# A decoder layer's second cross-attention stream: the query tiles of a quad are taken in the order 0, 7, 1, 6, 2, 5, 3, 4

## What is computed

```python
x = _layernorm(x + _L0_attn_ref(x, wq, wk, wv, wo, rel_emb))     # 16 heads of 64, relative bias
x = _layernorm(x + _L0_xattn_ref(x, ctx, ctx, Wq, bq, Wk, bk, Wv, bv, Er))
x = _layernorm(x + _L0_ffn_ref(x, Wg, bg, w1, b1, w2, b2, w3, b3))  # 16 experts, 128 tokens each
```

```python
QEr = jnp.einsum('bhsd,ld->bhsl', q, Er_s)
Srel = _skew(QEr)
QK = jnp.einsum('bhsd,bhtd->bhst', q, k)
attn = (QK + Srel) / math.sqrt(dh)
attn = jnp.where(causal[None, None], attn, -jnp.inf)
attn = jax.nn.softmax(attn, axis=-1)
out = jnp.einsum('bhst,bhtd->bhsd', attn, v)
```

## Time and profile before

| | us |
|---|---|
| median of three runs | 4421.03 |
| the profiled execution | 4421.36 |
| its span | 4419.6 |
| second stream in the first batch, from its first scores | 704.9 to about 909.6 |
| its quads 1 to 4 by windows | 54.6, 48.0, 48.1, 48.0 |

### The profile page before, as it was taken

How to read it: one execution, slowest core, us unless ns; L and a number is a source line. 1 busy time by engine, 2 the same in 40 slices (tenths; PEclk the granted TensorE clock), 3 DMA queues, 4 the chain that set the end, 5 groups by cost and what they waited for, 6 DMA issues and landing times. The chain is left out here.

```text
span 4419.6 us, 90910 instructions
## 1 busy us (share of the span) xinstructions
PE 3878.7 (88%) x36922; PEld 2372.6 (54%) x36922; DVE 2499.9 (57%) x4789; ACT 1573.0 (36%) x3188; POOL 908.0 (21%) x1023
## 2 busy tenths in 40 slices
PE   6999987899999878999998789999988819999992
PEld 3667544556665346566653566766545504444441
DVE  3777435777773357777723677777246762222224
ACT  2444135744441357444413674444137600000000
POOL 2333101123330011233300112333001102222220
PEclk8999999999999989999999899999998959999996
DMA  8333258634332686333327853433278414454445
GB/s 252 109 90 90 87 222 308 201 104 113 90 85 86 261 293 196 94 109 96 98 76 285 283 168 112 119 95 106 77 281 278 152 60 121 109 132 116 130 114 171
DMA packets 286223, 659.45 MB, mean 149 GB/s; under 512 B 24336, under 2 KB 90816, under 8 KB 282576
## 3 DMA queue, kind: packets, MB, share of 16 engines
q1 hardware_dynamic: 270160, 616.08, 43.2%
q0 software_dynamic: 15344, 35.46, 4.2%
q10 hardware_dynamic: 320, 2.23, 0.1%
HBM read 384.84 MB, written 210.11 MB: 135 GB/s over the span
## 5 line engine op out<-in xcount | busy, mean ns | idle before, releaser
L504 ACT ACTIVATE sc<-sc,nmax 128x1024 f32<-128x1024 f32 x516 | 591.7, 1147 | 797.6 <-DVE nmax L730 797.2
L461 POOL TENSOR_SCALAR sc<-sc,pinv 128x1024 f32<-128x1024 f32 x516 | 577.4, 1120 | 1230.0 <-DVE pinv L738 1217.2
L860 DVE CUSTOM_DVE_ANT_0 sc<-psum,big 128x896 f32<-128x896 f32 (+7 forms) x512 | 362.1, 754 | 217.5 <-PE psum L1221 170.7
L1039 PE MATMUL psum<-pts,wct 32*64 32x256 f32 x8192 | 458.6, 376 | 3.9 <-issue 3.9
L1039 PE MATMUL psum<-xall,wct 32*64 32x256 f32 x8192 | 457.6, 376 | 0.0
L1024 PE MATMUL psum<-xt,w_all 128*128 128x256 f32 x1792 | 415.7, 385 | 23.4 <-PEq L1021 23.4
L504 ACT ACTIVATE sc<-sc,xmax 128x896 f32<-128x896 f32 (+7 forms) x512 | 394.1, 772 | 49.8 <-DVE xmax L860 45.4
L755 DVE STREAM_TRANSPOSE pts<-sc 128x1024 f32<-128x1024 f32 (+3 forms) x342 | 333.6, 975 | 131.4 <-PE psum L1039 87.6
L1024 PEld LDWEIGHTS psum<-xt,w_all 128*128 128x128 f32 x1792 | 332.5, 190 | 128.2 <-issue 66.8
L730 DVE CUSTOM_DVE_ANT_0 sc<-psum,table_a 128x1024 f32<-128x1024 f32 x258 | 312.5, 1211 | 130.1 <-PE psum L986 114.2
L1039 PEld LDWEIGHTS psum<-pts,wct 32*64 32x64 f32 x8192 | 309.5, 132 | 100.8 <-issue 49.9
(11 more groups left out here) (160 smaller groups left out, 5553.0 us busy)
## 6 DMA issues: line engine op xcount, KB each, us to landing
wct<-xall SPq DMA_DIRECT2D x576, 128.0 KB, 2.4
big<-skew_d SPq DMA_DIRECT2D x48, 1024.0 KB, 5.4
w_sb<-w_dram SPq DMA_DIRECT2D x48, 1024.0 KB, 5.4
big<-skew_d SPq DMA_DIRECT2D x48, 768.0 KB, 4.4
big<-skew_d SPq DMA_DIRECT2D x32, 896.0 KB, 4.6
big<-skew_d SPq DMA_DIRECT2D x32, 640.0 KB, 5.2
w_all<-wqkv_dram SPq DMA_DIRECT2D x33, 512.0 KB, 3.6
skew_d<-wct SPq DMA_DIRECT2D x8, 2048.0 KB, 8.1
```

Source lines behind the costliest of these rows:

```text
L461: pool.tensor_scalar(sc[k % 4][:, :], sc[k % 4][:, :], pinv[:, k % 4:k % 4 + 1], 1.0, ALU.mult, ALU.mult).then_inc(probs_scaled, 1)
L504: act.activation(tile, tile, ACT.Exp, bias=least, scale=-1.0, accum_out=total).then_inc(probs_ready, 1)
L860: dve.tensor_tensor_reduce(scx[u % 2][:, at], SCORES[:, at], skw[u % 4][:, at], -XSCALE, BIG, ALU.add, ALU.min, xmax[:, k:k + 1]).then_inc ...
L1039: mm = pe.matmul(OSUM[HEAD[h], a, :], v_all[rows, ST * (b % GROUPS) + b // GROUPS, HEAD[h]], ptf[h][rows, QG * b:QG * b + QG], start=(b == ...
```

## The change

The constant `ORDER` sets the order of the tiles in each quad. A quad now runs t0, t7a, t7b, t1, t6a, t6b, t2, t5a, t5b, t3, t4a, t4b. All that is indexed by the tile's place in the sequence follows: which buffers a tile uses, when it is added, when its row statistics are taken. The wait for the swapped copy moves to the first unit that needs it, which is now the second of a quad and no longer the fifth. The first stream, and what SyncE does at which unit number, stay as they are.

```diff
+ORDER = [0, 7, 1, 6, 2, 5, 3, 4]
+UNITS = [(qd, t, hs) for qd in range(QUADS) for t in ORDER
          for hs in ([(0, 1, 2, 3)] if t < ST // 2 else [(0, 1), (2, 3)])]
...
+LAST = [max(i for i, u in enumerate(UNITS) if u[:2] == (v // ST, ORDER[v % ST])) for v in range(XV)]
...
-                    cols = xr[:, v % ST, P * (v // ST):P * (v // ST) + P]
+                    cols = xr[:, ORDER[v % ST], P * (v // ST):P * (v // ST) + P]
...
-                    m, v = TURN0[u] + g, UNITS[u][0] * ST + t
+                    m, v = TURN0[u] + g, UNITS[u][0] * ST + ORDER.index(t)
...
-                    if len(heads) == 2 and UNITS[u - 1][1] == t - 1 and t == ST // 2:
+                    if t == ORDER[1] and heads[0] == 0:
                         pe.wait_ge(swap_loaded[qd % 3], 64 * (qd // 3 + 1))
...
-                    qd, t = v // ST, v % ST
+                    qd, t = v // ST, ORDER[v % ST]
```

More of the change, by code:

```diff
@@ L53 @@
 ON_ACT = [a == 0 or (a, qd) == (1, 0) for a, qd in BLOCKS]
-UNITS = [(qd, t, hs) for qd in range(QUADS) for t in range(ST)
+ORDER = [0, 7, 1, 6, 2, 5, 3, 4]
+UNITS = [(qd, t, hs) for qd in range(QUADS) for t in ORDER
          for hs in ([(0, 1, 2, 3)] if t < ST // 2 else [(0, 1), (2, 3)])]
@@ L59 @@
 TURN0 = [sum(TURNS[:i]) for i in range(NU + 1)]
-LAST = [max(i for i, u in enumerate(UNITS) if u[:2] == (v // ST, v % ST)) for v in range(XV)]
+LAST = [max(i for i, u in enumerate(UNITS) if u[:2] == (v // ST, ORDER[v % ST])) for v in range(XV)]
 XSCALE = float(DH) ** -0.5
@@ L889, in _, with row_stats @@
                 dve.wait_ge(rel_stored[0], 16 * len(range(0, XV, 3)))
-                def row_stats(t):
-                    dve.wait_ge(x_added, XV - ST + t + 1)
+                def row_stats(i, t):
+                    dve.wait_ge(x_added, XV - ST + i + 1)
                     dve.bn_stats(stats[:, t, :], xr[:, t, :])
                 for u in range(NU + 7):
-                    for t in range(ST):
-                        if LAST[XV - ST + t] + 7 == u:
-                            row_stats(t)
+                    for i, t in enumerate(ORDER):
+                        if LAST[XV - ST + i] + 7 == u:
+                            row_stats(i, t)
                     if u < NU:
```

## The result

The new order is slower. The kernel before takes 4425.37 us (median of 5 runs, 4416.50 to 4429.57), the changed one 4447.25 (5 runs, 4443.01 to 4449.91); the ratio is 1.0050, 95% interval 1.0036 to 1.0065. That is 22 us more, with 6.5 either way. The forecast was 4428, its range 4402 to 4447: the result lies just outside.

A forecast was written before the change was run, and what follows sets the result against it. No engine was taken as full; the engines wait for one another. Opening +3.85, three quads at -0.25 and end -1.3 make +1.8 us a batch, +7.2 in all: 4428 us, 8 in 10 range 4402 to 4447.

The forecast's parts named there:

- The neighbours in a quad: Steady quad: same work, steps meet other neighbours; four locked steps again, new bank waits in t7b, t1 and t2.
- locked steps: Steps where TensorE's weighing waits until VectorE has done additions, one copy and the scaling of the tile before.
- The prices: Costs of weighing, transposes, additions and copies, read from the trace; steady quad 47.77 us against 48.02, -0.25 a quad.
- The clock: Steady quads: idle time no longer gathers in two neighbouring steps, so no fall; +0.8 us a quad if it falls.
- the first rival: The clock falls in every quad, each of 16 paying 1.05 us: 4445; chance 0.20.
- The opening: Each batch's first quad: t7a waits for the swapped copy; quad ends at 763.4 against 759.55, +3.85 us a batch.
- The rival of late loads: Opening quad: wide units now stand early and their loads come late, 3 us a batch: 4440; chance 0.10.
- The prediction's sum for the loads: Opening quad: units 2 to 5 need 3.8 MB where they needed 3.0.
- The end: Behind a batch's last scores: with t4b last, 10 transposes and 1.23 us of weighing, -1.3 us a batch.
- The sum: Whole kernel: 3.85 - 0.75 - 1.3 = +1.8 us a batch, +7.2 over four batches, 4428.
- The range: Whole kernel: forecast's own range 4416 to 4440; for 8 in 10, 4402 to 4447.

The follow-up runs named there:

- first_quad_old: New order, but each batch's first quad in the old order 0 to 7: 4429.79 us against 4421.98 for the kernel before, ratio 1.0017.
- late_load: New order with t7a's early load taken out of the first stream and issued behind the first swapped copy: 4449.05 us, ratio 1.0068 to the kernel before.
- scale_first_before: Kernel before (old order) with VectorE scaling a finished tile ahead of the step's copies: 4379.96 us against 4426.12, ratio 0.9897.
- early_loads_scale_first: Kernel before (old order) with t2's and t3's loads ahead of the swapped copy and scaling ahead of the copies: 4358.05 us, ratio 0.9851.
- early_loads: Kernel before (old order) with the loads of t2 and t3 issued ahead of the swapped copy: 4401.08 us against 4421.56, ratio 0.9954.

## Why the prediction was wrong

The reading held and sizes failed. In its own order:

- *The neighbours in a quad.* Right but for one: four locked steps, and new waits for a bank in t7b, t1 and t2 as named; the fourth, in t6b, stands ahead of the lock there and was not seen. All twelve steps are within 0.2 us.
- *The prices.* This step failed, and it is the largest part of the miss. Eight of the twelve steps lie above the forecast, by 0.83 together, and the quad is 48.57 for 47.77. Take t7b: the copy starts 3.49 us after the scores, as worked out. Then it takes 0.74 until TensorE goes on (775.19 to 775.93), not 0.61 + 0.08: 0.61 is VectorE's step to its next instruction, while who waits for the copy waits for its whole 0.69 and 0.05 of handing over. And the four last transposes take 0.59 to the weighing, not 0.43: the 0.17 marked "issue". The prediction had that 0.17 in t1 and t2 and left it out in t7b, t6a, t6b and t4a, and had half of it in t5a, whose own terms (1.07, 1.3 and 1.66) add up to 4.03 and not 4.10. The sign of the term turned: -0.25 a quad forecast, +0.55 measured.
- *The clock.* Right in eleven of the twelve quads behind the opening ones. The windows of quads 2 and 3 show 1.00, 2.4 GHz, where before showed 0.96 with a fall to 0.50. In the second quad of batch 2 it fell; windows of the changed kernel there:

```profile
1650.70:1654.10 3.40, 1.88 (x24) 1.18 (x24) 2.47 (x6) 2.40 (x5) 0.70 (x2) 1.00 0.75 234
1654.10:1657.50 3.40, 3.40 (x21) 3.07 (x19) 2.84 (x12) 2.28 (x8) 0.86 (x2) 0.50 0.68 194
```

  The first stretch holds the wait ahead of the fourth turn in t7b's step, the second is t1, which takes 4.25 for 3.44. That is the place that the first rival named, but it came once and not 16 times, and cost 0.8 us. The rule named there (the Trainium skill, "TensorE: Matmul & The Clock Gate", "A second HAM failure mode: psum-queue depth-cycling") agrees with the trace in this one quad and not in the other eleven: waits of 0.4 to 1.5 us in seven of the twelve steps left the clock up there. The time came out where the rival had put it, for another reason. The prediction's sentence that its sum for the quad would lose the 1.05 us of the fall is empty, as the sum has no fall in it.
- *The opening.* Right in mechanism, short in size. t7a's scores start 4.24 after the issue of the swapped copy (forecast 4.3) and 10.37 after t0 (10.44). t7a and t7b take 4.57 and 6.12 (4.62 and 5.97, with 1.0 for the low clock in each). The quad is 59.04, where 58.44 was forecast; the 0.6 is again the steps' prices. Over the four batches the opening quads cost 17.2, forecast 15.4. *first_quad_old* shows the 15 in the time itself.
- *Loads.* The rival of late loads did not come about: t7a waits for the swapped copy, and VectorE in the whole opening quad for TensorE alone (24.0 us in 11 waits), not for a mask. *late_load* shows what lateness looks like (t7a 6.46). The prediction's sum for the loads was off: t7b, t1, t6a and t6b need 3.25 MB, not 3.8.
- *The end.* Right: -1.5 a batch, forecast -1.3.
- *The sum.* Forecast +7.2, stream +18.4. Of the 11 us between, twelve quads at 0.8 make 9.6 and the opening 1.8; the quad of batch 2 in which the clock fell (49.37) adds 0.8, and the end takes 0.8 off. The runs of before have their median at 4425.37, 4 above that of the first three. That makes 4444; the 3 to 4 us that remain are inside the interval and, by the profiled executions, outside the stream. None of these runs settles them.
- *The range.* The prediction wrote that twelve steps at 0.1 or 0.2 each, 16 times over, are ±12 us, as if the errors went either way. They came of two prices used in every step, so they had one sign.

So the change was no gain because, of what it was meant to mix, nothing goes away: the quad has as many locked steps as before, the parity of the turns moved, and the second unit now needs the one input that is last to come.

## What to carry to other kernels

Before reordering units, count the waits between engines in a quad and ask which the order can remove; a small instruction that frees a bank, set ahead of a 0.69 us copy on the same engine, was worth 46 us here (some 13 of them the clock's, 1.05 in each of twelve quads), and the order alone, with all else mended, 0.64 us a quad. Where engines or banks go round by number, a new order changes who serves whom: look at that apart from the order. Price a wait by the whole duration of what it waits for plus the handing over, not by the step to that engine's next instruction, and price the first pass of a loop by itself, from what is last to come.

## What the runs showed of the hardware

- A wait of TensorE for a VectorE copy ends 0.05 us behind the copy's end (775.88, 775.93), and a group of matmuls behind transposes starts 0.17 later although what it waits for is done ("issue").
- 512 KB more of loads in the first stream, where the transfers share time with the stores, cost nothing that can be told (ratio 1.0004, 0.9995 to 1.0013), while t7a's load issued behind the swapped copy cost 2.4 us in the opening quad (61.85 on average for 59.49).
- The clock's fall goes with idle time that gathers, but not every time. Before, it fell once in each of the twelve quads behind the opening ones; with 0.6 us less of waiting in each of t2 and t3 (*scale_first_before*, *early_loads_scale_first*) in none of 24. In *early_loads*, where those waits are as before, it fell in ten of twelve, and in two of these it came earlier (769.20 to 772.60), inside t3's wait, and cost nothing: quad 46.95, t4a 4.42. Windows of *scale_first_before* behind the waits, which answer to the earlier trace rows:

```profile
771.50:775.00 3.50, 2.26 (x33) 1.78 (x29) 3.34 (x11) 2.42 (x7) 0.52 (x2) 1.00 0.57 221
775.00:778.50 3.50, 3.50 (x45) 2.56 (x45) 2.94 (x8) 2.99 (x9) 0.72 (x2) 1.00 0.76 227
```

TensorE is busy for 2.26 us of the first stretch, where it was 1.56 of 3.40, and the second, full one runs at 1.00 where it ran at 0.50.
